# One block for attention and experts, a one-hot slot table, down products four tiles behind up

## The chip, the cores and the metric

The kernel runs on one core of one Trainium2 chip. The metric is the device time of one execution in microseconds; a lower time is better. Profiles show one execution; their times count from the first instruction.

## The reference

A small language-model tower: a token embedding as a mixture of 4 basis vectors, one attention layer, one layer of 8 experts of which each token uses 2. There are 4 x 1024 tokens of width 256.

```
h = softmax(coeff[x]) @ (base + lang_bias) * 16 + lang_bias[2] * 0.1
p = layernorm(h) @ Wv.T + bv               # 16 heads of 16, q = k = v = p
h = h + (softmax(p p.T / 4) p) @ Wo.T + bo
x = layernorm(h);  top 2 of x @ router, weights = softmax of the two logits
for each token and chosen expert e:
    gate, up = split(x @ w13[e], 512)
    h = h + weight * ((silu(gate) * up) @ w2[e])
```

## The kernel before

All five engines run programs written by hand, with semaphores between them. There is no scheduler: the order on each engine is the order of the code.

**Attention** (`attention`, first block). The work is 16 groups: 4 batches by 4 sets of 4 heads. A group has 64 score tiles of 128 x 512, taken in 16 "quads" of four. PE makes the scores (`scores`, L335), ACT their exponentials (L701), PE the weighted sums (`sums`, L347). Between quads PE does small work for the group before (`after(quad)`, by the quad's number `at`): `fold` and `turn` bring the sums of a group into shape, `tile_rows` (L390, L391) makes two tiles of 128 token rows with their router logits, `rank` (L405, L406) counts how many tokens chose each expert so far. DVE takes these results: `fold_out`, `place_blocks`, `copy_rows` (L757), `choose` (L763 to L771), `normalise` (L776 to L793, 21 small operations on two columns), `normal_rows` (L800 to L803: the normalised rows, their 16-bit half and the rest), `weigh` (L808 to L810), `rank_read_out` (L815 to L817) and `places_out` (L822 to L833: a place number for each of the group's 512 token-expert pairs). DVE copies a group's sums at L1141.

POOL writes each pair's number to its place in a table in DRAM, `slots`, by four indirect stores a group (`note`, L586). It also splits the experts' weights into a high and a low bf16 part: ACT or POOL casts the high part (`high` L675, L649), POOL subtracts for the low part (`low`, L580). Weight pieces are loaded by SP into three buffers; 19 of 24 are done during attention, 5 after the last scores. SP stores the attention output to `out` and the normalised rows with their weights to `xrows` (L249, L254), by group.

**After the last scores.** DVE ranks and places the last group, and `tiles_out` (L837 to L853) works out where each expert's tiles of 128 slots begin. POOL notes the last group, then reads the table back (L661). PE turns it (L575), DVE makes the indices `idx_tok` and `second` (L1161 to L1164). `near_out` and `flags_out` make the flag `more`, which says whether the usual 68 tiles and two scatters in flight are enough, and the expert of each tile (L856 to L864). The block ends.

**Experts** (`experts`, second block). DVE clears the row buffers (L1443). There are 68 tiles of 128 slots, handled in four buffers `k`, 4 tiles to a pass of a loop. For tile j: POOL gathers rows (L1319), SP turns them by DMA transpose (`turn_x`, L1297), PE makes 12 products of 512 columns (`up`, L1368), ACT SiLU (L1404), DVE the weight (L1428), the product (L1432), its bf16 half (L1435) and the rest (L1437). SP turns each of the two by a DMA transpose of 128 x 512 (`turn_hidden`, L1302 and L1305). PE makes 12 products of 256 columns (`down`, L1377), ACT copies (L1409), POOL adds the rows to `out` by an indirect DMA (L1335), waiting for the scatter two before. PE's order in the loop is down(j), up(j+3), and it waits for the transposed rows of tile j+3 before down(j):

```
now = expert(j)
pe.wait_ge(hT_in[k], 32 * i + 32)
if not last or k == 0:
    coming = expert(j + 3)
    pe.wait_ge(xT_in[nk], 16 * (i + (k + 3) // XBUF) + 16)
down(k, j, now)
if not last or k == 0:
    up(nk, j + 3, coming)
```

POOL gathers tile j+4 when up(j) is done. Before all this each engine loads `flag`, which would start a second, safer version of the whole program (not taken here).

## Time and profile before

| | us |
|---|---|
| median of 3 runs | 930.94 (925.63 to 952.58) |
| profiled execution | 920.17 |
| its span, first to last instruction | 918.0 |
| PE busy | 761.0 (83%) |
| DVE, ACT, POOL busy | 522.5, 546.1, 360.5 |
| mean granted TensorE clock | 0.933 |

A row of the timeline has the start in us, the duration, the engine, line and operation, what is written from what, and how many instructions are merged; in brackets stands the idle time before it and what ended it. PEld rows are weight loads, which overlap PE. SPq rows are what SP needs to issue a DMA, not the transfer.

### The profile page before, as it was taken

What the parts mean: (1) busy time and instruction counts of PE and PEld (TensorE: products, weight loads), DVE (VectorE), ACT (ScalarE), POOL (GpSimd) and SP (SyncE); (2) the same over time, 40 slices, a digit from 0 to 9 for tenths busy, and PEclk for the clock granted to TensorE, in tenths of its full rate; (3) what the DMA queues carried; (4) which work ended last, traced back from release to release, by engine and by line L of the source; (5) the groups of instructions that cost most, each with busy time, mean ns of one, the idle gap of its engine ahead of it and who ended that gap; (6) DMA issues with size and microseconds to landing.
All of it is one profiled execution on the core that took longest, in us unless ns stands there. A gap on an engine that the chain in (4) does not pass through costs nothing. (4 is left out here: it accounts for less than half of the span.)

```text
span 918.0 us, 16662 instructions
## 1 busy us (share of the span) xinstructions
PE 761.0 (83%) x5175; PEld 294.6 (32%) x5225; DVE 522.5 (57%) x1613; ACT 546.1 (59%) x510; POOL 360.5 (39%) x309
## 2 busy tenths in 40 slices
PE   3499996988899899989988994058999999999991
PEld 2132221222222222222222221024555555555551
DVE  6734573557776657675656467733555555555540
ACT  0368995899999999999999993112222222222220
POOL 7660030321431133133311344334666666675752
PEclk9589996899999999999999997579999999999996
DMA  1030103012101110111011114146889889898872
GB/s 38 1 90 2 35 12 35 13 36 70 46 13 36 47 47 13 59 47 47 14 35 47 48 34 120 44 90 122 155 152 154 159 156 160 154 160 152 157 122 38
DMA packets 144722, 67.98 MB, mean 74 GB/s; under 512 B 118182, under 2 KB 140344, under 8 KB 144654
## 3 DMA queue, kind: packets, MB, share of 16 engines
q1 hardware_dynamic: 128494, 49.60, 23.8%
q0 software_dynamic: 16160, 17.55, 12.8%
q8 instruction: 34, 0.56, 0.3%
q14 instruction: 34, 0.28, 0.1%
HBM read 22.52 MB, written 17.57 MB: 44 GB/s over the span
## 5 line engine op out<-in xcount | busy, mean ns | idle before, releaser
L701 ACT ACTIVATE shared<-PS 128x1536 f32<-128x1536 f32 x342 | 467.9, 1476 | 57.2 <-PE PS L335 47.7
L347 PE MATMUL PS<-shared,va 128*32 128x512 f32 x2048 | 279.8, 619 | 3.4 <-DVE room L1141 3.1
L586 POOL DMA_INDIRECT slots<-pair_no,room x64 | 63.3, 990 | 385.4 <-DVE room L827 370.8
L1368 PE MATMUL PS<-w_p,room 128*128 x782 | 188.9, 385 | 14.7 <-DMA room<-room 13.0
L335 PE MATMUL PS<-room,ak 32*128 32x512 bf16 x1024 | 132.3, 393 | 50.9 <-ACT shared L701 43.1
L1404 ACT ACTIVATE shared<-PS 128x512 f32<-128x512 f32 x68 | 40.6, 597 | 164.8 <-PE PS L1368 164.8
L1432 DVE SCALAR_TENSOR_TENSOR shared<-shared,room,PS 128x512 f32<-128x512 f32 x68 | 50.8, 748 | 137.0 <-ACT shared L1404 137.0
L1335 POOL DMA_INDIRECT out<-room,idx_tok x68 | 112.5, 1654 | 34.4 <-issue 19.0
L1377 PE MATMUL PS<-shared,room 128*128 x816 | 102.8, 276 | 20.6 <-issue 13.4
L1368 PEld LDWEIGHTS PS<-w_p,room 128*128 128x128 f16 x816 | 80.9, 99 | 98.0 <-issue 18.2
L1319 POOL DMA_INDIRECT room<-xrows,idx_tok x68 | 71.8, 1055 | 101.2 <-PE PS L1368 76.5
L335 PEld LDWEIGHTS PS<-room,ak 32*128 32x128 bf16 x1024 | 31.8, 91 | 205.1 <-ACT shared L701 150.7
L1377 PEld LDWEIGHTS PS<-shared,room 128*128 128x128 bf16 x816 | 75.4, 98 | 57.5 <-issue 45.7
L1409 ACT COPY room<-PS 128x256 f32<-128x256 f32 x68 | 25.3, 372 | 76.2 <-PE PS L1377 76.2
L347 PEld LDWEIGHTS PS<-shared,va 128*32 128x32 f32 x2048 | 40.7, 109 | 68.0 <-issue 54.4
L1437 DVE TENSOR_TENSOR room<-shared,room 128x512 bf16<-128x512 f32 x68 | 50.7, 746 | 2.4
L757 DVE COPY room<-PS 128x264 f32<-128x264 f32 x32 | 13.8, 432 | 65.9 <-PE PS L391 65.9
L1435 DVE CAST room<-shared 128x512 bf16<-128x512 f32 x68 | 35.4, 521 | 2.3
L593 POOL DMA_INDIRECT cw<-coeff,xi x32 | 31.1, 973 | 10.8 <-issue 9.1
L580 POOL TENSOR_TENSOR w_p<-room,w_p 128x1024 bf16<-128x1024 f32 x16 | 34.2, 2136 | 1.4
L720 DVE CAST room<-PS 128x512 bf16<-128x512 f32 x32 | 22.0, 688 | 18.9 <-remote 17.2
L728 DVE SCALAR_TENSOR_TENSOR room<-room,part_c 128x512 bf16<-128x512 bf16 x32 | 25.8, 806 | 1.1
(257 smaller groups left out, 602.6 us busy)
## 6 DMA issues: line engine op xcount, KB each, us to landing
room<-w SPq DMA_DIRECT2D x24, 512.0 KB, 4.6
xrows<-room SPq DMA_DIRECT2D x16, 258.0 KB, 3.0
out<-room SPq DMA_DIRECT2D x16, 256.0 KB
room<-room SPq DMA_TRANSPOSE x204, 3.5
room<-xrows,idx_tok POOLq DMA_INDIRECT x68, 3.2
out<-room,idx_tok POOLq DMA_INDIRECT x68
slots<-pair_no,room POOLq DMA_INDIRECT x64, 6.4
xT<-xT SPq DMA_DIRECT2D x3, 256.0 KB, 5.8
```

Of the source, the lines that this page charges most:

```text
L335: last = pe.matmul(PS[:, WIDE * (u % BUFS) + i, :], g.ak[r, k0:k0 + P], qf[r, grp % 2, 512 * c:512 * c + 512], start=True, stop=True)
L347: last = pe.matmul(PS[32 * slot:32 * slot + 32, ACC, :], g.va[:, KT * (grp // HG) + kt, c, :], prob[:, (4 * quad + slot) % (RING * WIDE), ...
L586: pool.indirect_dma_start(g.slots, bass.IndirectOffsetOnAxis(pos_i[:, grp % 2, 2 * k + kk:2 * k + kk + 1].bitcast(U32), 0), g.pair_no[:, t ...
L701: act.activation(prob[:, at:at + n, :].rearrange("p n q -> p (n q)"), PS[:, buf:buf + n, :].rearrange("p c q -> p (c q)"), ACT.Exp).then_i ...
L1319: pool.indirect_dma_start(xs_w[:, j % XBUF, :], None, g.xrows, bass.IndirectOffsetOnAxis(g.idx_tok[:, j:j + 1].bitcast(U32), 0), bounds_ch ...
L1335: pool.indirect_dma_start(out, bass.IndirectOffsetOnAxis(g.idx_tok[:, m:m + 1].bitcast(U32), 0), y_s[:, m % XBUF, :], None, bounds_check=T ...
L1368: last = pe.matmul(PS[:, up_bank(k) + half, :], xsT[:, k, 2 * a + c, :], g.w13_p[:, w, c, ds(e, 1), FF * half:FF * half + FF].rearrange("p ...
L1377: last = pe.matmul(PS[:, YB[k % 2], 0:D], hidT[:, k, 4 * a + c, :], g.w2_p[:, w, c, ds(e, 1), :].rearrange("p e d -> p (e d)"), start=n == ...
L1404: act.activation(act_s[:], PS[:, up_bank(k), :], ACT.Silu).then_inc(silu_done, 1)
L1432: dve.scalar_tensor_tensor(hid[:], act_s[:], weight[:, k % 2:k % 2 + 1], PS[:, up_bank(k) + 1, :], ALU.mult, ALU.mult).then_inc(hid_ready, 1)
L1435: dve.tensor_copy(halves[:, k, 0], hid[:]).then_inc(split_step, 1)
L1437: dve.tensor_tensor(halves[:, k, 1], hid[:], halves[:, k, 0], ALU.subtract).then_inc(hid_split, 1)
```

## The change

1. **One block.** Attention and experts run in one block, one program behind the other; the load of `flag` moves behind the experts. The row buffers are cleared (`rows_cleared`) and the SiLU table is loaded during attention. Engines wait for new semaphores: POOL gathers after `idx_ready` and all stores, PE starts after `flags_ready` and 16 low parts, the loops after `flags_ready` 2.
2. **Last slots by one-hot products.** The last group's places are not stored to DRAM. `last_slots` makes for each of its four columns of pairs a one-hot of the row and one of the tile (scaled by pair number less 16384, the blank's value), and PE adds the four products to the turned table in PSUM (`slot_table`).
3. **Last group's order.** `rank(14)` moves from quad 14 to quad 10, the second `tile_rows` from 7 to 6; DVE ranks, places and normalises group 14 before the last sums' copy, and writes its rows behind it. The last group's two row products go to two banks together, its normalised rows are written by ACT. The slots come before `near_out` and `flags_out`. The last two low parts (`lows_left`) stand behind the first four gathers.
4. **Experts.** PE starts with four up products, and its order is down(j), up(j+4); both halves of a tile go through one DMA transpose of 128 x 1024, ahead of which SP waits for both. The last tile is turned by PE (`turn_last`), and ACT and DVE split it behind that.

```diff
+        def last_rows():
+            pe.wait_ge(z_placed, LAST + 1)
+            for kk in range(2):
+                t = tile_of(LAST, kk)
+                pe.matmul(PS[:, kk, 0:DE], z_blk[:, LAST % 2, kk, :], g.pair[:, t % KT, :], start=False, stop=True).then_inc(h_mm, 1)
+
+        def slot_table():
+            pe.wait_ge(hot_ready, 1)
+            for k in range(4):
+                pe.matmul(PS[:, 0, 0:ECOLS], row_hot[:, k, :], tile_hot[:, k, :], start=k == 0, stop=False)
+            pe.wait_ge(table_copied, 1)
+            pe.matmul(PS[:, 0, 0:ECOLS], table_f[:], g.ident[:, 0:ECOLS], start=False, stop=True).then_inc(table_turned, 1)
...
-            if at == 14 and grp >= 1:
+            if at == (10 if grp == LAST else 14) and grp >= 1:
                 rank(grp - 1)
...
         for n in range(BESIDE, BESIDE + WB):
             low(n)
-        note(GROUPS - 1)
-        for n in range(BESIDE + WB, len(pieces)):
-            low(n)
         pool.wait_ge(row_ready, 1)
         for k in range(2):
-            pool.wait_ge(noted[k], 64 * (GROUPS // 2))
+            pool.wait_ge(noted[k], 64 * ((GROUPS - k) // 2))
...
+        def last_slots():
+            link(dve.tensor_scalar(at_row_i[:], pos_i[:, LAST % 2, :], P - 1, None, ALU.bitwise_and))
+            dve.tensor_copy(at_row[:], at_row_i[:])
+            firsts = prod[:].rearrange("p k (t e) -> p (k t) e", e=E)
+            link(dve.tensor_tensor(firsts, picked[:], first[3][:].unsqueeze(1).to_broadcast([P, 4, E]), ALU.mult))
+            link(dve.reduce_sum(at_tile[:], firsts, X))
+            link(dve.tensor_tensor(at_tile[:], at_tile[:], apart_f[:], ALU.add))
+            for k in range(4):
+                dve.tensor_scalar(row_hot[:, k, :], g.iota_r[:], at_row[:, k:k + 1], None, ALU.is_equal)
+                hot = dve.tensor_scalar(tile_hot[:, k, :], g.iota_r[:, 0:ECOLS], at_tile[:, k:k + 1],
+                                        late_no[:, k // 2, k % 2:k % 2 + 1], ALU.is_equal, ALU.mult)
+            hot.then_inc(hot_ready, 1)
...
         def turn_hidden(k, j):
-            sp.wait_ge(split_step, j + 1)
-            sp.sem_inc(sp_step, 1)
-            sp.dma_start_transpose(hidT[:, k, 0:4], halves[:, k, 0]).then_inc(hT_in[k], 16)
             sp.wait_ge(hid_split, j + 1)
             sp.sem_inc(sp_step, 1)
-            sp.dma_start_transpose(hidT[:, k, 4:8], halves[:, k, 1]).then_inc(hT_in[k], 16)
+            sp.dma_start_transpose(hidT[:, k], halves[:, k].rearrange("p a f -> p (a f)")).then_inc(hT_in[k], 16)
...
-                pe.wait_ge(hT_in[k], 32 * i + 32)
-                if not last or k == 0:
-                    coming = expert(j + 3)
-                    pe.wait_ge(xT_in[nk], 16 * (i + (k + 3) // XBUF) + 16)
+                if last and k == XBUF - 1:
+                    pe.wait_ge(lo_ready, 1)
+                else:
+                    pe.wait_ge(hT_in[k], 16 * i + 16)
+                if not last:
+                    coming = expert(j + XBUF)
+                    pe.wait_ge(xT_in[k], 16 * i + 32)
                 down(k, j, now)
-                if not last or k == 0:
-                    up(nk, j + 3, coming)
+                if not last:
+                    up(k, j + XBUF, coming)
+                elif k == 0:
+                    turn_last(j + XBUF - 1)
```

On DVE, behind the copy of the last sums (L1141, after the change L1222), stood the places of group 14 (L822 to L833) and the fold (L735). Before:

```order
L1141 TENSOR_SCALAR room<-PS 128x512
L822 TENSOR_TENSOR room<-room 128x32
L824 TENSOR_REDUCE room<-room 128x4
L827 CAST room<-room 128x4
L830 TENSOR_TENSOR room<-room 128x16
L831 TENSOR_SCALAR room<-room 128x4
L832 CAST room<-room 128x4
L833 TENSOR_TENSOR room<-room 128x2
L735 RECIPROCAL room<-PS 128x32
```

And after the change:

```order
L837 SCALAR_TENSOR_TENSOR room<-room 128x2
L1222 TENSOR_SCALAR room<-PS 128x512
L846 TENSOR_SCALAR room<-room 128x256 x2
L848 CAST room<-room 128x2x256
L849 TENSOR_TENSOR room<-room 128x2x256
L779 RECIPROCAL room<-PS 128x32
```

The places have moved ahead of the copy, and the row copies of group 14, which stood ahead of it, now stand between the copy and the fold. On DVE, where the slots are made, the indices were the last thing in the block. Before:

```order
L872 TENSOR_REDUCE room<-room 128x1
L856 TENSOR_TENSOR room<-iota_r,room 1x518
L858 TENSOR_REDUCE room<-room 1x74
...
L864 TENSOR_SCALAR more<-room 1x1
L1159 CAST room<-room 128x128
L1161 TENSOR_TENSOR room<-PS,spare_row 128x74
L1162 TENSOR_SCALAR idx_tok<-room 128x74
```

And after, behind the last of the eight one-hot operations (L863, L864):

```order
L864 TENSOR_SCALAR room<-iota_r,room 128x74
L1238 CAST room<-room 128x128
L925 TENSOR_TENSOR room<-iota_r,room 1x518
L927 TENSOR_REDUCE room<-room 1x74
L928 CAST tile_expert<-room 1x1
L929 CAST tile_expert<-room 1x74
L939 TENSOR_TENSOR room<-PS,spare_row 128x74
L940 TENSOR_SCALAR idx_tok<-room 128x74
L941 TENSOR_SCALAR room<-room 128x74
L942 CAST second<-room 128x74
L945 TENSOR_TENSOR room<-room 128x256
```

The indices have moved ahead of `near_out` (L945) and the flags, but stay behind the experts of the tiles. On SP, one tile of the expert loop, before:

```order
L1302 DMA_TRANSPOSE room<-room 128x4x128
L1305 DMA_TRANSPOSE room<-room 128x4x128
L1295 ISA
L1297 DMA_TRANSPOSE room<-room 128x4x128
L1300 REGISTER_ALU
```

And after:

```order
L1383 DMA_TRANSPOSE room<-room 128x8x128
L1376 ISA
L1378 DMA_TRANSPOSE room<-room 128x4x128
L1381 REGISTER_ALU
L1383 DMA_TRANSPOSE room<-room 128x8x128
```

Two transposes of 128 x 512 for the hidden rows have become one of 128 x 1024; the transpose of the next rows stands behind it as before.

## Rows read from the trace of the kernel before

**Rows 1.** Page, part 4: the chain that ended last, by line.
```profile
PE PS L1368 17%; PE PS L1377 10%; DMA room<-room 2%; SPq L1302 1%; SPq L1305 0%; SPq L1297 0%; DMA room<-xrows,idx_tok 0%; ACT shared L1404 0%; DVE shared L1432 0%; DVE room L1435 0%; POOL out L1335 0%; DVEq L1527 0%; DVE room L1443 0%; ACT room L1409 0%; DVEq L1283 0%
```

**Rows 2.** Windows view: PE, PEld, DVE, ACT, POOL busy, clock, DMA share, GB/s.
```profile
618.00:893.00 275.00, 260.57 (x1526) 148.08 (x1560) 141.35 (x257) 62.39 (x129) 171.85 (x126) 0.99 0.86 151
```

**Rows 3.** Timeline, 586 to 619 us: from the table's gather to the first down product.
```profile
586.11 1.20 POOL L661 DMA_INDIRECT room<-slots,room  x1 [4.12 <-DMA slots<-pair_no,room]
...
592.69 0.20 DVE L1162 TENSOR_SCALAR idx_tok<-room 128x74 int32<-128x74 int32 x1
...
596.73 0.92 DVE L1443 MEMSET room<- 128x1032 f32 x1 [3.50 <-issue]
598.48 1.02 POOL L1319 DMA_INDIRECT room<-xrows,idx_tok  x1 [11.18 <-DVE room L1443]
...
605.36 9.96 PE L1368 MATMUL PS<-w_p,room 128*128 x35 [12.98 <-DMA room<-room]
...
618.10 1.50 PE L1377 MATMUL PS<-shared,room 128*128 x12 [2.78 <-issue]
```

**Rows 4.** Timeline, 892 to 906 us: the last tiles.
```profile
892.19 1.54 POOL L1335 DMA_INDIRECT out<-room,idx_tok  x1 [2.97 <-DMA out<-room,idx_tok]
...
893.43 1.47 PE L1377 MATMUL PS<-shared,room 128*128 x12
...
901.63 2.74 PE L1377 MATMUL PS<-shared,room 128*128 x12 [4.26 <-DMA room<-room]
...
905.56 1.54 POOL L1335 DMA_INDIRECT out<-room,idx_tok  x1 [5.46 <-ACT room L1409]
```

**Rows 5.** Chain in order of time: start, duration, what; a tile without a wait.
```profile
676.92 1.32 PE PS L1377 x12
678.25 2.59 PE PS L1368 x12
```

**Rows 6.** Timeline, 878 to 890 us: one tile from up to down.
```profile
878.21 2.75 PE L1368 MATMUL PS<-w_p,room 128*128 x12
...
883.02 0.69 DVE L1437 TENSOR_TENSOR room<-shared,room 128x512 bf16<-128x512 f32 x1
...
883.88 1.19 SPq L1302 DMA_TRANSPOSE room<-room  x1
...
885.18 1.23 SPq L1305 DMA_TRANSPOSE room<-room  x1
...
889.50 1.51 PE L1377 MATMUL PS<-shared,room 128*128 x12 [0.41 <-issue]
```

**Rows 7.** Timeline of SP, first and last of ten transposes.
```profile
870.11 1.19 SPq L1297 DMA_TRANSPOSE room<-room  x1
...
882.31 1.22 SPq L1297 DMA_TRANSPOSE room<-room  x1
```

**Rows 8.** Timelines of DVE, ACT and POOL, 557 to 586 us.
```profile
557.03 0.69 DVE L1141 TENSOR_SCALAR room<-PS 128x512 f32<-128x512 f32 x1
...
566.85 3.39 DVE L768 CAST room<-room 128x4 f32<-128x4 uint32 x1
...
572.88 0.17 DVE L837 TENSOR_TENSOR room<-room,expert_base 128x8 f32<-128x8 f32 x1
...
576.03 0.75 DVE L776 BATCH_NORM_STATS2 room<-room 128x6 f32<-128x256 f32 x2
...
577.16 4.85 DVE L781 TENSOR_TENSOR room<-room 128x2 f32<-128x2 f32 x1
...
585.17 0.74 DVE L800 TENSOR_SCALAR room<-room 128x256 f32<-128x256 f32 x2
...
557.03 3.16 ACT L675 CAST shared<-room 128x1024 bf16<-128x1024 f32 x3 [1.10 <-PE PS L347]
...
563.94 6.27 POOL L580 TENSOR_TENSOR shared<-room,shared 128x1024 bf16<-128x1024 f32 x3
...
577.79 4.20 POOL L580 TENSOR_TENSOR shared<-room,shared 128x1024 bf16<-128x1024 f32 x2
```

## Prediction before the change ran

> **What bounds the kernel now.** I first looked for the chain that ended last. The reader sees two matrix lines carry it, the up product (L1368, 17% of the span) and the down product (L1377, 10%) [rows 1]. So the expert stage is read first, then the stretch before it. From 618 to 893 us the timeline has 260.6 us of PE work in 275.0 us at a granted clock of 0.99, with the DMA engines at 0.86 [rows 2]. The first down product starts at 618.10 [rows 3], the one of tile 65 at 893.43 [rows 4]: 65 tiles at 4.24 us. Where nothing is waited for, down takes 1.32 us and up 2.59 us, 3.91 us a tile [rows 5]. So 0.33 us a tile is lost to something that is not arithmetic.
>
> One tile shows what it is [rows 6]. Its up product starts at 878.21 and ends near 880.9; the difference of the two halves at 883.02, the transposes at 883.88 and 885.18, and its down product at 889.50. That is 8.6 us from the end of up to the start of down, and with down three tiles behind up only two tiles of other work (7.8 us) lie between. A full turn is 8.6 plus a down and an up (3.9), 12.5 us for three tiles: 4.2 us, the rate seen. The SP queue is a second bound close by: from 870.11 to 882.31 ten transposes start, each 1.36 us behind the last [rows 7], so three a tile take 4.07 us. PE comes third, with 3.91.
>
> Between attention and experts PE does almost nothing from 557 to 605.36. DVE runs the chain there. It copies the last sums at 557.03; stands 3.39 us in a cast of 4 elements while POOL does three weight subtractions (563.94 for 6.27 us); starts on tile counts at 572.88; stands 4.85 us in a 2-element product beside two more subtractions (577.79 for 4.20); and ends the normalising at 585.17 [rows 8]. The slots are ready at 592.69, the rows are cleared only at 596.73, in the next block, the first gather goes at 598.48, and the first up product at 605.36 [rows 3]. At the end the last up product is finished at about 893.4; three down products are left, the first at 893.43, the last at 901.63, held 4.26 us by its transpose, and its scatter starts at 905.56. After that come 12.5 us to the span's end at 918.0 [rows 4].
>
> **The change, part by part.** The profiled execution took 920.17 us for a span of 918.03. Sums are in its times.
>
> Attention's last group. The ranks of group 14 move ahead of the end of the scores; its notes go out earlier and leave POOL free at the end. But the row copies of group 14 (L800 to L803) now stand right behind the copy at 557.03, just where POOL's three subtractions will begin: ACT's three casts for them start at 557.03 and take 3.16 in all [rows 8], so the first subtraction starts near 558.1. Before, these three met a cast of 4 elements; now they meet a cast or a two-input difference at about 558.5. I take it that DVE again stands until all three are through: 558.1 + 6.3 = 564.4. Then come the rest of the copies, the fold, the turned blocks and the rows, with both tiles' products together instead of one behind the other (1.5 to 2.5 us less), and the choice: the ranks at 570.7 to 571.5, as now. I count this part at nothing. If the starvation does not come, it is worth up to 5; if it grows, it costs some 3. The clearing of 1032 columns (0.92 us in rows 3) and the residual products ahead of the fold lie in waits of DVE and PE and cost nothing; without that cover 0.9 and 0.7.
>
> The Trainium skill, page "SBUF — State Buffer", section "SBUF: two separate sides", says that DVE and GpSimd take a shared port pair as an exclusive lock for one whole instruction, and that a DVE operation with two SBUF inputs or in a two-port mode needs it. By that rule DVE would get in after one subtraction, about 2 us, and the part would be worth some 3 us. The rows agree that it blocks, but not with the one instruction: 3.39 and 4.85 us are longer than one subtraction of 2.1 [rows 8]. The measurement decides, and the rule is a rival below.
>
> From the ranks to the first gather, now 571.5 to 598.48, 27.0 us. After: tile counts 3.2 (572.88 to 576.03) make 574.7. Normalising 4.3 (576.03 to 585.17 less the stall of 4.85) makes 579.0; POOL has no subtraction now, since the last two stand behind the gathers. ACT then writes the normalised rows and their half; DVE needs 0.74 for the first two of these [rows 8], I take 1.8 for ACT's three, with the places of group 15 beside it on DVE: 580.8. The difference and the weights 1.3: 582.1. One-hot rows: 13 DVE operations at 0.18, the mean of the normalising's (4.3 us for 20, partly linked): 2.3, so 584.4. The cast of the table and the experts of the tiles stand ahead of the slots: 0.2 + 2.0. The five small products on PE hide beside them. The slots, 0.4: 587.0. The table itself is read from 574.8 on, no longer behind the last four notes (now 586.11), so it has landed. The gather follows at once, since rows are cleared and no block ends: 587.1. That is 11.4 us earlier, and the stored rows, sent at 582.1, have 5 us to land. Bounds: DVE a little faster and no starvation, 16; a late store or an ACT table load in the chain, 7. I take 11.4.
>
> Filling the experts' pipeline. From first gather to first up stays 6.9: 594.0. Four ups in place of three before the first down add 2.6 at most; the gathered x(4) must now land before down(0) and stands on SP behind the merged transpose. I put the first down 14.6 us behind the first up, where it was 12.7: 608.6. POOL's two subtractions (4.2 us) lie between its fourth and fifth gather, beside the first up product; without that cover they cost 2.
>
> The steady stage. Down is four tiles behind up, so three tiles of work, 11.7 us, lie between the end of up and the start of down. The way there: the merged transpose can start only when both halves are there (3.0 us after up ends), then SP needs it, then x(j+4), which PE also waits for before down(j). The trace has no transpose of 1024 columns. Bounds: 1.2 us if an instruction costs the same whatever its size, 2.7 if it costs two whole starts. I take 2.4, twice 1.2 without the second gap. SP then needs 2.4 + 0.16 + 1.36 = 3.92 a tile, as PE does. Landing: the lo transpose was issued at 885.18 and down started 4.3 later [rows 6], so x(j+4) is there 3.0 + 2.6 + 4.3 = 9.9, up to 10.5, after up ends, under 11.7. So PE becomes the bound at 3.91, and with two streams of equal length side by side I take 3.97. 64 periods (one fewer, since one more up is done ahead) are 254.1: the last up ends, and down(64) starts, at 862.7. ACT, DVE and POOL have 1.0, 2.2 and 2.6 us of work a tile (62.4, 141.4 and 171.9 us [rows 2] over 65) and stay covered; POOL's scatter now waits for a y of the same period, 0.3 us at most on the following gather, inside the slack.
>
> The tail. After the last up: down(64), the four turns of tile 67 on PE, 65, 66, then its own: 1.4 + 0.9 + 1.4 + a wait of 0.5 for the transpose of 66 + 1.4 + 1.4, some 7.1 us, where it took 10.9 (893.43 to 904.4). Scatters then crowd: each waits for the one two before, as the one at 892.19 waited 2.97 us [rows 4], so the last one starts 9.8 behind the last up, where it was 12.1: 872.5. Then 12.5 as now, and one load of the flag that has moved behind the stage, 1.0 to 1.2: 886.1.
>
> Sum: gather 11.4, stage 288.1 (605.36 to 893.43) less 268.7 = 19.4, tail 2.3, flag -1.1: 32.0. The execution becomes 888.2. The median of the runs shown is 930.94, 10.8 above the profiled execution; taking 32.0 from it gives 898.9, my forecast 899. A difference of about 2% (912.3) is what a measurement of this kernel can tell from none.
>
> **Rivals.**
> (A) SP or the DMA engines stay the bound. If a merged transpose costs its 2.7, SP needs 4.07 a tile; if the 16 engines can't go beyond 0.95 busy, the 0.86 of a tile of 4.24 us allows no less than 3.84, and at 0.90 4.05. At 4.07 the stage gives back 6.4: 905. For it speaks that the starts were 1.36 apart while the queue was full; against it, that one of two fixed gaps goes. The Trainium skill, page "DMA: Bandwidth & Descriptors", section "Bandwidth", puts the ceiling between SBUF and DMA at 435 GB/s; the stage moves 151 [rows 2], so by bytes nothing would hold it, and the sum would stay 899. The busy share of 0.86 says otherwise, and I keep the rival.
> (B) The lock is for one instruction, so the last group is shorter by 3: 896.
> (C) The added wait decides. If x(j+4) lands later than 11.7 us after up(j), because merged packets stand before it and its gather, a turn is 3.9 plus that: at 13.5 us, 4.35 a tile, which gives back 24: 923. It decides from 11.7 on; my 9.9 to 10.5 leave little over a microsecond.
> (D) Slower than before: the transpose of 1024 columns costs much more than two of 512 on SP. From 2.95 us the gain of 32 is gone (period 4.47); at 3.4 the period is 4.92 and the time 960. Nothing in the rows speaks for it but that this size does not occur.
> (E) The one-hot table does not shorten anything since another input of the gather is late (the stored rows of group 15): 11.4 shrinks to 5, 905.
>
> **How the numbers follow.** Forecast 0.52, A 0.20, B 0.10, C 0.07, D 0.04, E 0.07. The predicted time is the forecast's 899. The range: downward the period of 3.91 and the whole 16 us of the first part give 8 less, and runs of the same kernel lie 5 below their median: 886. Upward A and E together give 912, and with 5 for runs above their median 917; that leaves C and D out. Faster by over 2%: forecast, A, B and E, less what scatter takes from A and E, 0.87. C falls within 2%, with that scatter: 0.09. Slower: D, 0.04.
>
> **What would show it.** In the changed profile: the first gather near 587 and the first up near 594; DVE standing 5 to 6 us from 558.5 beside three subtractions (if only 2, B); SP rows of the merged transpose near 2.4 us, and starts of down 3.9 to 4.0 apart without a gap in PE; the last up near 863, the last scatter near 872.5. If the merged row is 2.7 or more, A or D; if PE waits for x's transpose before down while SP is idle, C. The prediction is wrong if the period stays above 4.1 or the gather starts after 592.

## The result, and the profile after

The changed kernel takes 900.2 us (median of four executions, 898.6 to 901.6) where the kernel before takes 928.7 (925.6 to 952.6): a ratio of 0.970, with a 95% interval of 0.966 to 0.975. It is faster by about 3%. The forecast was 899. Some executions are over 1.5% slower than the fastest of the same kernel, as the one of 952.6 is here; the ratios and all medians from here on leave them out, which puts the kernel before at 926.4 us.

The profiled executions differ by less, 920.17 and 900.00 us. The chain that ended last is carried by the same two products, up (now L1450) and down (L1459), as in [rows 1], but the waits beside them are other ones:

```profile
PE PS L1450 19%; PE PS L359 15%; ACT shared L736 15%; PE PS L1459 10%; PE PS L347 7%; PE PS L402 2%; PE PS L379 2%; PE PS L403 1%; PE PS L445 1%; DMA room<-room 1%; DMA out<-room,idx_tok 1%; PE PS L386 0%; DVE room L766 0%; PE PS L492 0%
```

The windows view of the expert stage, from the first down product to the 65th (PE, PEld, DVE, ACT, POOL busy, clock, DMA share, GB/s), answers to [rows 2]: PE is at work in 253.1 of 261.0 us, where it was in 260.6 of 275.0.

```profile
613.90:874.90 261.00, 253.06 (x1505) 146.71 (x1538) 137.44 (x256) 61.44 (x127) 169.22 (x125) 1.00 0.96 157
```

The timeline of the changed kernel from the copy of the last sums to the end answers to [rows 3, 4, 8]:

```profile
562.82 0.69 DVE L1222 TENSOR_SCALAR room<-PS 128x512 f32<-128x512 f32 x1 [1.53 <-PE PS L359]
563.88 4.52 POOL L609 TENSOR_TENSOR shared<-room,shared 128x1024 bf16<-128x1024 f32 x2 [2.33 <-ACT shared L710]
564.19 2.23 DVE L848 CAST room<-room 128x512 f16<-128x512 f32 x1
566.45 2.49 DVE L849 TENSOR_TENSOR room<-room 128x512 f16<-128x512 f32 x1
...
576.34 0.17 DVE L906 TENSOR_TENSOR room<-room,expert_base 128x8 f32<-128x8 f32 x1
580.08 1.07 POOL L687 DMA_INDIRECT room<-slots,room  x1 [6.66 <-DVE room L922]
...
591.85 0.23 DVE L939 TENSOR_TENSOR room<-PS,spare_row 128x74 int32<-128x74 f32 x1 [0.40 <-PE PS L421]
592.12 0.20 DVE L940 TENSOR_SCALAR idx_tok<-room 128x74 int32<-128x74 int32 x1
593.26 1.03 POOL L1399 DMA_INDIRECT room<-xrows,idx_tok  x1 [12.11 <-DVE idx_tok L940]
...
600.04 1.06 PE L1450 MATMUL PS<-w_p,room 128*128 x2 [5.31 <-DMA room<-room]
613.87 1.39 PE L1459 MATMUL PS<-shared,room 128*128 x11 [1.02 <-DMA room<-room]
...
874.89 1.36 PE L1459 MATMUL PS<-shared,room 128*128 x11
...
886.01 1.54 POOL L1416 DMA_INDIRECT out<-room,idx_tok  x1 [1.77 <-DMA out<-room,idx_tok]
```

Cut at the same events in both traces, the 19.8 us between the spans (918.0 and 898.2) come out like this. Down(64), the 65th, starts at 889.5 before.

| stretch | before | after | difference |
|---|---|---|---|
| start to the copy of the last sums | 557.0 | 562.8 | +5.8 |
| copy to first gather | 41.4 | 30.4 | -11.0 |
| first gather to first down | 19.6 | 20.6 | +1.0 |
| 64 intervals between downs | 271.4 | 261.0 | -10.4 |
| down(64) to the end | 28.5 | 23.4 | -5.2 |

### The profile page after: what moved, and what is told of

It is laid out like the page before. It is cut to its first block, busy times and chain, and to the rows that moved or that the text cites. A ratio compares the mean times of both kernels' runs of the same rounds, so it can differ in the third digit from the quotient of the medians.

```text
span 898.2 us, 16552 instructions
## 1 busy us (share of the span) xinstructions
PE 755.5 (84%) x5189; PEld 296.1 (33%) x5238; DVE 515.3 (57%) x1623; ACT 548.4 (61%) x515; POOL 355.8 (40%) x305
## 4 chain that ended last, share of the span: by engine, by line
PE 60%; ACT 15%; issue 11%; DVE 8%; another core or an unknown queue 2%; DMA 2%; SPq 0%; POOL 0%; ACTq 0%; DVEq 0%; POOLq 0%
PE PS L1450 19%; PE PS L359 15%; ACT shared L736 15%; PE PS L1459 10%; PE PS L347 7%; PE PS L402 2%; PE PS L379 2%; PE PS L403 1%; PE PS L445 1%; DMA room<-room 1%; DMA out<-room,idx_tok 1%; PE PS L386 0%; DVE room L766 0%; PE PS L492 0%
## 5 line engine op out<-in xcount | busy, mean ns | idle before, releaser
L615 POOL DMA_INDIRECT slots<-pair_no,room x60 | 59.6, 993 | 374.4 <-DVE room L895 360.7
L1450 PE MATMUL PS<-w_p,room 128*128 x783 | 184.7, 383 | 7.0 <-DMA room<-room 5.3
L1450 PEld LDWEIGHTS PS<-w_p,room 128*128 128x128 f16 x816 | 80.4, 99 | 89.4 <-issue 8.5
L1459 PE MATMUL PS<-shared,room 128*128 x816 | 101.3, 273 | 8.3 <-issue 6.9
L1459 PEld LDWEIGHTS PS<-shared,room 128*128 128x128 bf16 x816 | 75.9, 97 | 41.3 <-issue 27.8
L1538 DVE TENSOR_TENSOR room<-shared,room 128x512 bf16<-128x512 f32 x67 | 46.4, 693 | 2.3
L622 POOL DMA_INDIRECT cw<-coeff,xi x32 | 31.2, 976 | 10.8 <-issue 9.2
```

The lines of the kernel that those rows point to most:

```text
L615: pool.indirect_dma_start(g.slots, bass.IndirectOffsetOnAxis(pos_i[:, grp % 2, 2 * k + kk:2 * k + kk + 1].bitcast(U32), 0), g.pair_no[:, t ...
L1450: last = pe.matmul(PS[:, up_bank(k) + half, :], xsT[:, k, 2 * a + c, :], g.w13_p[:, w, c, ds(e, 1), FF * half:FF * half + FF].rearrange("p ...
L1459: last = pe.matmul(PS[:, YB[k % 2], 0:D], hidT[:, k, 4 * a + c, :], g.w2_p[:, w, c, ds(e, 1), :].rearrange("p e d -> p (e d)"), start=n == ...
L1538: dve.tensor_tensor(halves[:, k, 1], hid[:], halves[:, k, 0], ALU.subtract).then_inc(hid_split, 1)
```

## The experiments

Each run was timed beside the kernel before on the same chip, with four executions as a rule: e0 to e3 on one chip, e4 to e7 on a second, the last four on a third. The changed kernel itself was not run on the second, so e4 to e7 have no time of it beside them and are judged by their parts against its profiles elsewhere; the chip of the first comparison is not on record. The table has the median, that of the kernel before beside it, and from the trace: the copy of the last sums, copy to first gather, mean interval of the first 65 downs, and the mean of the intervals that end where a pass of four tiles ends ("fourth") and of the rest.

| run | us | before | copy at | to gather | interval | fourth / others |
|---|---|---|---|---|---|---|
| before (first profile) | 926.4 | | 557.0 | 41.4 | 4.24 | 4.53 / 4.14 |
| changed (first profile) | 900.2 | 926.4 | 562.8 | 30.4 | 4.08 | 4.41 / 3.97 |
| e0_after_again | 888.5 | 921.2 | 555.6 | 28.7 | 4.06 | 4.35 / 3.97 |
| e1_two_turns | 894.9 | 921.2 | 553.8 | 30.4 | 4.15 | 4.40 / 4.07 |
| e2_lag3 | 902.9 | 921.2 | 557.6 | 30.4 | 4.30 | 4.41 / 4.26 |
| e3_unroll2 | 890.3 | 921.2 | 557.2 | 30.4 | 4.06 | 4.30 / 3.98 |
| e4_no_scatter | 892.1 (one) | 924.1 | 562.9 | 30.4 | 3.93 | 3.98 / 3.92 |
| e5_two_blocks | 904.1 | 924.1 | 562.8 | 38.5 | 4.07 | 4.40 / 3.96 |
| e6_rows_ahead | 894.7 | 924.1 | 561.8 | 27.7 | 4.06 | 4.36 / 3.96 |
| e7_note_last | 901.2 | 924.1 | 560.2 | 33.4 | 4.08 | 4.40 / 3.97 |
| b0_before_again | 949.8 | 953.6 | 564.9 | 40.3 | 4.67 | 4.94 / 4.58 |
| e9_gather_early | 897.9 | 953.6 | 562.1 | 30.4 | 4.08 | 4.42 / 3.97 |
| e10_after_mark | 899.4 | 954.8 | 563.2 | 30.4 | 4.09 | 4.40 / 3.99 |
| e11_flat_ahead | 888.5 | 954.8 | 564.1 | 26.1 | 3.95 | 3.94 / 3.96 |

**The changed kernel again.** Edit: none.

> The changed kernel itself, once more, as the mark for the others of this call. Its four executions so far lay between 898.6 and 901.6 us, so 900 +- 1.5 is expected. It also shows whether the part that the change does not touch varies from profile to profile: the first exponentials on ACT began at 41.45 us here and at 37.92 in the profile of the kernel before, and the copy of the last sums stood at 562.82 against 557.03. Theory 1 (how long the first part takes varies by execution): the copy stands up to 6 us elsewhere this time, and the time moves with it. Theory 2 (the change in the code itself delays it): it stands within 1 us of 562.8 again.

Theory 1 holds: the copy stood at 555.55, 7.3 us earlier, with the code unchanged, and the time fell to 888.5. Of the 11.3 us between the two spans 7.3 are that; 1.7 lie between copy and first gather, the rest behind it. Over all profiles the copy lies between 553.8 and 564.9, and it goes mostly by the chip: 553.8 to 557.6 on the first, 560.2 to 562.9 on the second, 562.1 to 564.9 on the third, where the kernel before has the 564.9 and the changed one 563.2. Nothing in this speaks for the 5.8 us of the first comparison being an effect of the change. The ratio to the kernel before was 0.966 (0.959 to 0.974).

**Distance and merging apart.** Two transposes for the hidden rows, with four tiles of distance:

```diff
-            sp.wait_ge(hid_split, j + 1)
-            sp.dma_start_transpose(hidT[:, k], halves[:, k].rearrange("p a f -> p (a f)")).then_inc(hT_in[k], 16)
+            sp.wait_ge(split_step, j + 1)
+            sp.dma_start_transpose(hidT[:, k, 0:4], halves[:, k, 0]).then_inc(hT_in[k], 16)
+            sp.wait_ge(hid_split, j + 1)
+            sp.dma_start_transpose(hidT[:, k, 4:8], halves[:, k, 1]).then_inc(hT_in[k], 16)
```

> The changed kernel with SP's transpose of the hidden rows in two again (512 columns each), all else as changed, four tiles of distance included. Theory 1 (SP's time for a transpose goes by the instruction: 1.19 us for 512 columns, 1.23 for 1024): SP has three transposes a tile again, about 3.9 us, as much as PE's 3.90, so it can no longer catch up after a turn of the loop; the stage lasts 64 x 4.15 in place of 64 x 4.08, 904 to 906 us in all. Theory 2 (the distance of four tiles alone took away the waits, the merging gave nothing): 900 +- 1.5.

The interval is 4.15 and the time 894.9, 6.4 us above the changed kernel on the same chip (64 intervals at 0.09 more are 5.7 of them). Theory 1 holds. PE waits here 8.6 us in all for x's transposed rows, whose transpose now stands third on SP, and 0.3 us in the changed kernel beside it. Then the distance alone was set back:

```diff
-                down(k, j, now)
-                if not last:
-                    up(k, j + XBUF, coming)
+                down(k, j, now)
+                if not last or k == 0:
+                    up(nk, j + 3, coming)
```

> The changed kernel with down three tiles behind up again (up of tile j+3 after down of tile j, last tile turned on TensorE after the second down of the last pass), all else as changed, one transpose for both halves included. Theory 1 (the merged transpose alone brings the halves in time, the fourth tile of distance only costs a first down 3.9 us later and gives it back at the end): 900 +- 2, periods as now. Theory 2 (three tiles are too short a distance for the chain of STT, cast, subtraction, transpose and transfer of 1024 columns): waits before down as in the kernel before, 0.1 to 0.2 us a tile, 906 to 913 us.

Theory 2 holds, more than I had put it: 4.30 an interval, where I had expected 0.1 to 0.2 above 4.08, and 902.9 us. PE waits 20.3 us in all for the transposed hidden rows, where it waits under 1 us with four tiles of distance. Merging the transposes shortens SP's work, but the first half then has to wait for the second, and three tiles of distance leave no room for that. Whether merging alone is worse than the kernel before (4.24 in its first profile) is not shown, since no profile of it is known to be from this chip. The waits view shows the same from SP's side, where the kernel before hardly waits for DVE's half of the hidden rows and the changed one waits for its difference (waiting line, releaser, us in total, times, longest), 625 to 880 us of the kernel before and then of the changed one:

```profile
SPq L1301 <- DVE room L1435: 4.4, 4, 2.4
```

```profile
SPq L1382 <- DVE room L1538: 40.9, 41, 2.6
```

An SP that waits 41 times for its input is no longer a bound. The timeline of SP in the changed kernel gives its reason, the merged transpose of 1024 columns first and x's of 512 second; they take the same time:

```profile
768.24 1.23 SPq L1383 DMA_TRANSPOSE room<-room  x1
770.70 1.19 SPq L1378 DMA_TRANSPOSE room<-room  x1
```

**Is the rest the turn of the loop, or the transfers?**

```diff
-        with eng.Fori(0, USUAL // XBUF - 1) as i:
-            body(i, False)
+        with eng.Fori(0, (USUAL // XBUF - 1) // 2) as i:
+            body(i * 2, False)
+            body(i * 2 + 1, False)
```

> The changed kernel with two passes of four tiles in one turn of the loop on every engine: 8 turns in place of 16. In the changed kernel every fourth interval between downs is 4.2 to 4.6 us where the others are 3.90 to 3.93 and a few 4.0 to 4.4. Theory 1 (the turn of the loop on PE costs about 0.5 us of its own): every second long interval goes, 8 x 0.5 = 4 us, 896 us. Theory 2 (the transfer engines, 0.96 busy in this stage, are the bound, and the long interval is only where PE catches the transfers up): the mean interval stays at 4.08, 900 +- 1.5.

The time did not fall (890.3 against 888.5, interval 4.06), which read like theory 2. The fourth intervals were shorter where no turn stands behind them (mean of eight 4.19) than where one does (mean of seven 4.47, or 4.35 without a single one of 5.20), but the gain did not show in the sum. So the scatters of the tiles 4 to 63 went, which leaves their rows out of the output:

```diff
             pool.wait_ge(y_copied, m + 1 + FREE)
+            if left_out(m, apart):
+                return
             pool.indirect_dma_start(out,
...
```

> The changed kernel without the accumulate scatters of the tiles 4 to 63 (60 of 68; waits and signals around them kept, so the output lacks what those tiles add). Transfers in the expert stage fall by the scattered rows, 128 KB a tile. Theory 1 (the transfer engines' share of 0.96 bounds the stage or causes the odd intervals of 4.0 to 4.4 us): the mean interval falls from 4.08 to below 3.97 and the time by 7 us or more. Theory 2 (a turn of the loop on PE makes the long intervals): every fourth interval stays at 4.2 to 4.6, the mean at 4.03 or more, the time falls by 3 us at most.

The interval of this one execution fell to 3.93, and even the fourth ones to 3.98, as theory 1 has it, although the 16 turns were still there. By its windows row PE is busy through the whole stage and the DMA share is 0.65:

```profile
613.30:864.87 251.57, 251.12 (x1537) 148.87 (x1538) 135.94 (x256) 61.62 (x127) 67.79 (x65) 1.00 0.65 132
```

Both runs spoke for the transfers, and I held the gathered rows that SP waits for (36.7 us in 42 waits in the changed kernel's second profile, 1.1 in this one) for the cause. The next edit sends the gathers out earlier:

```diff
                 pool.wait_ge(weighed, j - XBUF + 1)
-                pool.wait_ge(up_mm, j - XBUF + 1)
                 gather(j)
-                if j >= XBUF + 3:
-                    scatter(j - XBUF - 3, apart)
+                if j >= XBUF + 4:
+                    scatter(j - XBUF - 4, apart)
```

> The changed kernel with POOL's gather of tile j+4 no longer waiting for up of tile j (it waits only for the weights that were read from the same rows; SP's transpose of the new rows comes behind that of the hidden rows of tile j, and so behind up), and issued ahead of the scatter that stood in front of it. The gather goes out some 2 us earlier in each tile; transfers, bytes and everything else stay. Without the scatters SP waited 1.1 us in all for gathered rows, with them 36.7 us in 42 waits, and the mean interval fell from 4.07 to 3.93. Theory 1 (what stretches the intervals is that gathered rows come late behind the scatters on the same queue, and hold up SP's transposes): mean interval 3.95 +- 0.03, 7 us less than the changed kernel. Theory 2 (the transfer engines, 0.95 busy, are themselves the bound, in whatever order the transfers come): mean interval 4.04 to 4.08, time unchanged within 2 us.

It did to SP what it should: the waits view has no wait for gathered rows left, only this one.

```profile
SPq L1382 <- DVE room L1537: 39.2, 32, 1.8
```

And it did nothing to the interval, 4.08. Late rows were not the cause. "The transfer engines are the bound" was left, and the last run took that down as well. It writes the loop out in full, with the edit of e6_rows_ahead (below) beside it:

```diff
-        with eng.Fori(0, USUAL // XBUF - 1) as i:
+        for i in range(USUAL // XBUF - 1):
             body(i, False)
```

> The changed kernel once more, as the mark for the other run of this call: 885 to 902 us as on the chips so far, 30.4 us from the copy of the last sums to the first gather (28.7 where the cast beside POOL's subtraction does not wait), mean interval between downs 4.06 to 4.08 us.

> The changed kernel with the normalised rows of the group before the last ahead of the copy of the last sums (worth 2.7 us between copy and first gather in the run with that edit alone), and with the expert loop written out in full: no turn, no register in a wait. In every trace the interval from the fourth tile of a pass to the next is the long one (4.30 to 4.42 against 3.97), even in the passes of the doubled loop that have no turn behind them; without the scatters it was 3.98. Theory 1 (the register arithmetic at the start of a pass is what makes it long where nothing hides it): the fourth intervals come down to those of the others, mean 3.96 to 3.98, 6 us less, together 9 us under the mark. Theory 2 (the transfer engines set the mean, and the start of a pass is only where PE waits for them): the mean stays at 4.04 to 4.08, the same waiting spread over other tiles, 2.7 us under the mark; fetching the longer program adds at most 1 us.

The time is 888.5 (887.3 to 889.1) against 899.4 (894.5 to 900.2) of the changed kernel on the same chip. Of the 11.4 us between the two spans, 4.4 lie between copy and first gather and 8.9 in the 64 intervals (3.95 against 4.09); 0.9 is lost in a later copy of the sums and 1.0 in the filling and the end. The fourth intervals are gone. All transfers are still there, and they show a share of 1.06, so 0.96 was no ceiling:

```profile
610.36:863.41 253.05, 250.75 (x1507) 147.93 (x1537) 140.55 (x256) 61.65 (x128) 172.41 (x125) 1.00 1.06 164
```

**What the expert stage is bound by.** In most tiles PE's own queue of register instructions, in the others PE's products. In the changed kernel the timeline shows a fourth interval, 773.03 to 777.65, that ends in an idle time put down to nothing ("issue"):

```profile
773.03 1.47 PE L1459 MATMUL PS<-shared,room 128*128 x12
774.34 2.75 PE L1450 MATMUL PS<-w_p,room 128*128 x12
777.65 1.50 PE L1459 MATMUL PS<-shared,room 128*128 x12 [0.56 <-issue]
```

The trace also records the queue's instructions (start, us, line, operation). In the same interval, the products and some short rows left out:

```
772.90 0.051 L1459 FUSED_REGOPS    first of 16, 0.12 us apart: addresses of the expert's weights
774.80 0.046 L1450 FUSED_REGOPS    the last of them
774.93 0.032 L1365 ALU_OP          turn of the loop
775.02 0.214 L1365 COMPARE_BRANCH
775.29 0.068 L1365 FUSED_REGOPS
775.42 0.677 L1442 TENSOR_LOAD     expert of tile j
776.16 0.151 L1442 FUSED_REGOPS
776.65 0.306 L1442 TENSOR_LOAD     expert of tile j+4
777.01 0.156 L1442 FUSED_REGOPS
777.44 0.051 L1456 EVENT_SEMAPHORE
777.55 0.046 L1459 FUSED_REGOPS    first of the next down, which starts at 777.65
```

The queue hardly rests in these 4.65 us. Of the first 65 down products none starts sooner than 0.10 us after its first address operation, and 34 start 0.10 to 0.11 us after it, so those stood waiting for their address. The 16 address operations take 1.90 us from first to last. From the last to the next down's first it is 2.04 us where no turn lies between and 2.55 where one does (means of 47 and 16), 0.1 of it waiting for semaphores. That makes 3.94 and 4.45 a tile, 4.07 on average; the interval is 4.08. The two must agree, since the sum only cuts the interval in two; what it shows is that the queue works nearly all of it. The source view of the three lines, 640 to 860 us (min/median/max ns), has the pieces:

```profile
L1459 PEldq FUSED_REGOPS  x431: 46/46/51, 641.9 to 859.9; - x144
L1442 PEldq TENSOR_LOAD <-tile_expert x108: 296/320/935, 639.9 to 858.3; - x108
L1365 PEldq COMPARE_BRANCH  x14: 214/214/224, 644.0 to 856.7; - x14
```

No interval of any kernel is shorter than 3.90 us, which is what the products of a tile need. That gives a count for every run: how long the 64 intervals last beyond 64 x 3.90, how many of them stand at 3.90, and how long PE's queue waited in all for the transposed hidden rows and for x's (idle time ahead of the instruction with that wait, beyond the usual 0.06 us). All but the count is in us.

| run | beyond 64 x 3.90 | at 3.90 | hidden rows | x's rows |
|---|---|---|---|---|
| before (first profile) | 21.8 | 3 | 17.4 | 0.2 |
| b0_before_again | 49.4 | 5 | 41.6 | 0.2 |
| e2_lag3 | 25.4 | 3 | 20.3 | 0.3 |
| e1_two_turns | 16.2 | 4 | 0.6 | 8.6 |
| changed (first profile) | 11.4 | 16 | 1.1 | 0.0 |
| e10_after_mark | 12.3 | 13 | 1.1 | 0.0 |
| e4_no_scatter | 2.0 | 42 | 0.2 | 0.1 |
| e11_flat_ahead | 3.5 | 34 | 0.5 | 0.0 |

So the change took away PE's wait for the hidden rows. What is left in the changed kernel is hardly any wait for data but the queue's own work.

Without the scatters the two loads of a tile take 0.72 us, not 0.86, and the stretch 1.86, not 2.04: 3.77 a tile is less than the products' 3.90, the queue gets ahead by 0.13 a tile and has most of a turn's 0.5 in hand when it comes. With the loop in full the turns are gone and the loads take 1.02. Now 34 of 64 intervals stand at 3.90, so the products are the bound in over half of the tiles and longer loads in the rest. The doubled loop took out 8 turns, 4 us by this count, and its 64 intervals were 0.4 us shorter: its loads took 56.4 us in the stage where the changed kernel's took 54.2, and the rest is not explained. The turn's part is thus shown by an experiment, the loads' part only read from the traces. Why the loads take longer with more traffic and with denser issue stays open, and so does whether in the last run some of them wait for the products. A kernel with one load a tile in place of two was not tried.

**One block.**

```diff
+        with nc.Block() as block:
+            block.sync(sp_a)
...
         with nc.Block() as block:
-                again(sp, both(sp_a, sp_e), None, sp_r, both(sp_b, sp_f))
+                again(sp, sp_e, None, sp_r, both(sp_b, sp_f))
```

> The changed kernel with attention and experts in two blocks again, so that all engines meet between the last flag and the first gather; all else as changed, the cleared rows and the early Silu table included. Theory 1 (the meeting was what stood between indices and gather: 5.8 us before, 0.94 after): first gather 4 to 6 us after the indices, 904 to 906 us. Theory 2 (the moved clearing and table load were most of those 5.8 us): the first gather comes within 3 us of the indices, 902 us or less.

Theory 1 holds: 904.1 us, the first gather 38.5 us behind the copy and not 30.4. It comes 9.2 us behind the indices, more than the 4 to 6 expected, because the flags now end 2.9 us behind the indices and the meeting comes after them. The timeline shows the meeting: the flag, now worked out behind the indices (592.12 in this run too), is written at 594.98, and the gather goes 6.3 us after it.

```profile
594.98 0.14 DVE L935 TENSOR_SCALAR more<-room 1x1 int32<-1x1 f32 x1
601.27 1.02 POOL L1399 DMA_INDIRECT room<-xrows,idx_tok  x1 [20.12 <-issue]
```

**Rows ahead of the sums.**

```diff
+            if grp == LAST:
+                normal_rows(LAST - 1)
             dve.wait_ge(summed, GQUADS * (grp + 1))
...
-        normal_rows(LAST - 1)
         fold_out(LAST)
```

> The changed kernel with the normalised rows of the group before the last worked out ahead of the copy of the last sums, where DVE waits 1.5 us for PE, not behind it, where a cast and a subtraction took 2.23 and 2.49 us beside POOL's subtractions instead of 0.43 and 0.69. Theory 1 (those 5.4 us on DVE lie on the chain to the ranks): the chain from the copy of the last sums to the ranks is 4 to 5 us shorter, the copy 0.5 later, 896 to 897 us. Theory 2 (what comes next on DVE is then held up by POOL's subtractions in its place): 900 +- 1.5.

Copy to gather fell by 2.7 us, not by 4 to 5; the median is 894.7. Both theories have a part. The cast and the difference take 0.43 and 0.69 now, but a later cast of 4 elements meets the third subtraction and stands 1.64:

```profile
560.71 0.43 DVE L848 CAST room<-room 128x512 f16<-128x512 f32 x1
561.17 0.69 DVE L849 TENSOR_TENSOR room<-room 128x512 f16<-128x512 f32 x1
561.78 0.69 DVE L1224 TENSOR_SCALAR room<-PS 128x512 f32<-128x512 f32 x1
...
569.67 1.64 DVE L812 CAST room<-room 128x4 f32<-128x4 uint32 x1
...
569.16 2.12 POOL L609 TENSOR_TENSOR shared<-room,shared 128x1024 bf16<-128x1024 f32 x1 [2.74 <-ACT shared L710]
```

In the last run the three subtractions fell together, that cast took 0.17, and the gain was 4.4.

**One-hot products.**

```diff
-                pe.matmul(PS[:, 0, 0:ECOLS], row_hot[:, k, :], tile_hot[:, k, :], start=k == 0, stop=False)
...
+        note(LAST)
         pool.wait_ge(row_ready, 1)
...
-        last_slots()
```

> The changed kernel with the ranks of the last group written to the table by POOL's four scatters again, and the table read after them; the one-hot products left out, all else as changed. Theory 1 (the scatters land 8.3 us after the last of them was issued, as in the kernel before): ranks placed at 578, scatters issued to 583, landed at 591 to 592, indices 6.6 us later at 598, 6 us later than now: 905 to 907 us. Theory 2 (the scatters land sooner without POOL's subtractions behind them, and the one-hot products cost DVE and PE as much as the scatters did): indices at 592 +- 2, 900 +- 2.

Between the two theories: copy to gather 33.4, 2.9 us more, and 901.2 us. The scatters do land late, theory 1's 8.3 us after the last was issued being 7.6 here, but they were issued sooner than I had put them: by 580, not 583. And the one-hot products have a price of their own: DVE needs 2.6 us for them (586.64 to 589.26 in the changed kernel), where here it stands idle for 4.2 until the table is in:

```profile
579.00 0.97 POOL L612 DMA_INDIRECT slots<-pair_no,room  x1 [0.30 <-issue]
587.57 1.06 POOL L685 DMA_INDIRECT room<-slots,room  x1 [7.60 <-DMA slots<-pair_no,room]
590.11 0.23 DVE L1235 CAST room<-room 128x128 f32<-128x128 int32 x1 [4.21 <-DMA room<-slots,room]
592.47 0.20 DVE L938 TENSOR_SCALAR idx_tok<-room 128x74 int32<-128x74 int32 x1
```

**The kernel before again.** Edit: none.

> The kernel before itself, for a second profiled execution. The two first profiled executions differ by 20.2 us (920.2 and 900.0) while the medians differ by 28.5, and the kernel before spreads over 926 to 953 us where the changed one stays within 3 us. Theory 1 (the spread of the kernel before arises in its expert stage, whose mean interval between downs was 4.24 us in one execution and may be longer in others; three tiles of distance leave too little slack for late rows): this profile differs from the first in that interval, by 0.1 us for every 6.4 us of time, while the stretch from the copy of the last sums to the first gather stays 41 to 42 us. Theory 2 (the spread is that of the first part, the copy of the last sums standing at another time): the interval stays at 4.24 and the copy moves from 557 with the whole difference.

Theory 1 holds in the main. On this chip the kernel before takes 949.8 us, its interval is 4.67, and the copy to the gather is 40.3, 1.1 less. Of the 30.2 us between the two spans the 64 intervals make 27.6; the copy itself stands 7.8 us later, which is theory 2's part, and 5.3 are won back elsewhere. The timeline shows where: down waits for its transposes, issued at 762.88 and 764.18.

```profile
762.88 1.19 SPq L1302 DMA_TRANSPOSE room<-room  x1
764.18 1.20 SPq L1305 DMA_TRANSPOSE room<-room  x1
...
770.07 1.50 PE L1377 MATMUL PS<-shared,room 128*128 x12 [1.62 <-issue]
```

Second transpose to down is 5.9 us, where it was 4.3 in [rows 6], and PE's waits for the hidden rows come to 41.6 us, where they were 17.4. Why the transposes land later here is not known. The changed kernel stays at 4.09 on the same chip. So the change is worth 26.2, 32.7 and 55.3 us in the three comparisons, most on the chip where the kernel before was seen to wait longest.

## Why the prediction was right, and where it was not

- **The waits of the loop.** The reading of [rows 6] was right: the round trip of up, halves, transposes and down set the rate. PE's waits for the hidden rows fell from 17.4 us to 1.1. Undone, the distance costs 0.23 us a tile and the merging 0.09, each beside the other.
- **The period.** This is the term that was mis-sized: "So PE becomes the bound at 3.91, and with two streams of equal length side by side I take 3.97." It measured 4.08 here and 4.06 to 4.09 elsewhere, 6.9 us over the 64 intervals. SP's 3.92 was wrong as well: the merged transpose took 1.23 us, the lower of my bounds, so SP needs some 2.7 a tile. What stands in its place is PE's queue of register instructions, 3.94 a tile on average and 0.5 more at each turn of the loop; only 16 of the 64 intervals ran at the products' 3.90. It was there to be seen: every fourth interval was long in the kernel before too (4.53 against 4.14), and I read one tile and an average.
- **Rival A** gave exactly this period (4.07) for a wrong reason. Both causes it names fell: SP waits for its input, and the DMA share rose to 1.06 at 3.95. The Trainium skill's figure named there ("DMA: Bandwidth & Descriptors", section "Bandwidth"), by which the bytes hold nothing back, agrees: the same transfers went at 151 GB/s before, 157 after and 164 in the last run, each time faster.
- **Rivals C, D and E** fell: PE waits under 0.1 us in all for x's rows (and SP's wait for the gathers, taken away, changed nothing), the transpose is cheap, and the gather followed the indices by 1.1 us.
- **The last group**, counted as nothing: copy to tile counts took 13.5 us, not 15.9, but 1.3 of that is order (with the places ahead of the counts, as before, e7_note_last has 14.9), so the part was worth 1.0. "I take it that DVE again stands until all three are through" failed: it stood in two instructions, each until one subtraction was through (564.19 to 566.42 beside the first of 563.88). The Trainium skill's rule of one lock for one instruction ("SBUF — State Buffer", section "SBUF: two separate sides") agrees with these rows, though not with the 4.85 us of the kernel before, where one operation stood beside both subtractions [rows 8]; rival B had the mechanism. Its 3 us did not come whole, since two instructions were caught.
- **Ranks to gather.** Predicted 15.6 from the start of the counts, measured 16.9. The small products did not hide beside the table's work: DVE waited 0.40 for them at 591.85, and POOL's gather went 1.1 after the indices, not 0.1.
- **Filling and tail.** First gather to first down 20.6 (predicted 21.5), down(64) to the end 23.4 (23.4).
- **The total.** The measured span of 898.2 is 12.1 us above the predicted 886.1. By parts: 5.8 from the varying first part, 6.9 from the period, 0.4 and -0.9 from the rest. The forecast of the time held all the same because it started from the median of the kernel before, 10.8 above its profiled execution, while the changed kernel's profiled execution lies at its median. That the difference would go on unchanged was an assumption, not a reading. The size 899 is thus two errors that nearly cancel; the sign and its parts are what the traces bear out.

## What to carry to other kernels

Before calling the array or a queue the bound, add up the issuing queue of the busiest engine over one period, register loads, address arithmetic and loop turns included, and look at the intervals one by one: a long one at a fixed phase of the loop is hidden in an average, and the count of those at the shortest length shows how often the products are the bound. More distance between producer and consumer buys not only time but steadiness, since a short chain pays each slow transfer in full. And a test that makes the interval fall (leaving the scatters out) names a condition, not yet the cause.

## What the runs showed of the hardware

- SP's time for a DMA transpose goes by the instruction: 1.23 us for 1024 columns, 1.19 for 512.
- An address in a register costs PE's queue 0.12 us per operation and a turn of the loop 0.5 us. A load of one number from SBUF takes it 0.30 to 1.08 us: on average 0.36 without the scatters, 0.43 in the changed kernel, 0.51 with the loop in full.
- The DMA share of the windows view is no share of a capacity: it went to 1.06.
- Four indirect scatters of single words were still under way 7.6 us after the last was issued (8.3 in the kernel before).
- All engines meeting between two blocks: 6.3 us from the last flag to the first gather.
- The first part, up to the copy of the last sums, varied by chip more than by execution: it ended within 4 us on each of three chips (four profiles each) and between 553.8 and 564.9 us over all.
